# Small products in column tiles, a transfer of their own for search keys, and the next chunk's chain six ticks further forward

## What is computed

```python
xz = xseq @ in_proj_w; x, z = jnp.split(xz, 2, axis=-1)      # products xin, z
x = silu(conv1d(x))                                          # 4 taps per channel -> u
dt, Bm, Cm = split(x @ x_proj_w)                             # products dt, BC
delta = softplus(dt @ dt_proj_w + dt_proj_b)
h = exp(delta * A) * h + (delta * x) * Bm                    # the scan, 128 x 16 states
y = (einsum(h, Cm) + x * D) * silu(z) @ out_proj_w           # products y, out
# layer 1, on the image y
attn_c = softmax(xc @ xc.T); attn_s = softmax(q.T @ k)       # en; 4096 x 4096 scores
out = x + w_bn @ concat(attn_c @ x, v @ attn_s)
```

## Time and profile before

| | us |
|---|---|
| median of 3 runs | 8052.4 |
| lowest and highest | 8051.38, 8057.28 |
| the profiled execution | 8055.58 |
| its span, first to last instruction | 8053.8 |
| busy over the span: PE | 7258.6 (90%) |
| DVE | 6833.3 (85%) |
| ACT | 5958.7 (74%) |
| POOL | 3797.6 (47%) |

### The profile page before, as it was taken

The page is one execution under the profiler, slowest core; times in us unless marked ns, Lnnn a source line. Parts: engine busy times, 40 slices in busy tenths (PEclk is TensorE's granted clock), DMA queues, the critical chain, the costliest instruction groups (busy, mean ns, idle before and its releaser), DMA issues. The chain is left out here.

```text
span 8053.8 us, 226290 instructions
## 1 busy us (share of the span) xinstructions
PE 7258.6 (90%) x84718; PEld 2577.4 (32%) x84718; DVE 6833.3 (85%) x11132; ACT 5958.7 (74%) x10582; POOL 3797.6 (47%) x4135
## 2 busy tenths in 40 slices
PE   9972379999999999999989999999999999999998
PEld 2321123333333333333333333333333333333343
DVE  2228899898989899898989899898989899899987
ACT  1114478788888788887878788787878888788875
POOL 0016555555555455555545455555545455555500
PEclk9985589999999999999999999999999999999999
DMA  9838888888888888888888888878887888888820
GB/s 151 133 89 215 218 208 206 206 206 205 202 210 203 208 198 209 207 203 206 200 196 200 203 205 207 209 201 208 202 207 204 203 205 205 204 209 205 201 54 17
DMA packets 886811, 1535.68 MB, mean 191 GB/s; under 512 B 409480, under 2 KB 459472, under 8 KB 885712
## 3 DMA queue, kind: packets, MB, share of 16 engines
q1 hardware_dynamic: 882640, 1520.79, 78.3%
q10 hardware_dynamic: 3072, 0.40, 0.0%
HBM read 1326.69 MB, written 176.95 MB: 187 GB/s over the span
## 5 line engine op out<-in xcount | busy, mean ns | idle before, releaser
L1321 POOL TENSOR_TENSOR hst<-hst,cbc 128x512 f32<-128x512 f32 x2048 | 2623.1, 1281 | 2322.8 <-DVE bank L1179 2295.9
L1193 DVE TENSOR_TENSOR_SCAN hst<-dA,carry,bank 128x512 f32<-128x512 f32 x1792 | 2286.0, 1276 | 4.9 <-DVE bank L1179 0.4
L1044 ACT ACTIVATE pr<-bank 128x512 f32<-128x512 f32 x4096 | 2224.3, 602 | 36.7 <-PE bank L920 34.5
L931 PE MATMUL bank<-pr,vt 128*32 128x512 f32 x16384 | 2128.5, 595 | 2.3 <-DVE accs L1278 1.5
L1050 ACT ACTIVATE dA<-lanes,small 128x512 f32<-128x512 f32 x2048 | 1497.2, 731 | 645.7 <-DMA lanes<-spread_d 595.7
L917 PE MATMUL bank<-s1q,s1k 128*32 128x512 bf16 x16384 | 1626.6, 383 | 249.3 <-ACT pr L1044 151.1
L853 PE MATMUL bank<-s1kx,s1q 128*32 128x512 bf16 x16384 | 1641.2, 386 | 151.7 <-DMA s1kx<-kx_d 102.1
L986 ACT ACTIVATE gains<-bank 128x512 f32<-128x512 f32 x2048 | 1219.7, 596 | 650.0 <-PE bank L853 570.8
L1179 DVE TENSOR_TENSOR bank<-lanes,bbc 128x512 f32<-128x512 f32 x2048 | 1510.1, 737 | 200.2 <-DMA lanes<-spread_d 119.1
L920 PE MATMUL bank<-t2q,t2k 128*32 128x512 bf16 x16384 | 1616.5, 381 | 0.0
L1131 DVE CUSTOM_DVE_ANT_0 gains<-bank,gains 128x512 f32<-128x512 f32 x2048 | 1403.3, 685 | 210.6 <-PE bank L853 196.3
(11 more groups left out here) (120 smaller groups left out, 5757.9 us busy)
## 6 DMA issues: line engine op xcount, KB each, us to landing
lanes<-spread_d SPq DMA_DIRECT2D x2048, 512.0 KB, 6.3
seqt<-seq_d SPq DMA_DIRECT2D x256, 128.0 KB, 4.8
spread_d<-dsp SPq DMA_DIRECT2D x128, 256.0 KB, 2.0
spread_d<-usp SPq DMA_DIRECT2D x128, 256.0 KB, 2.0
bbc<-bc_d SPq DMA_DIRECT2D x128, 256.0 KB, 3.4
cbc<-bc_d SPq DMA_DIRECT2D x128, 256.0 KB, 4.0
xpad<-in_x SPq DMA_DIRECT2D x64, 256.0 KB, 6.7
ypad<-ypad SPq DMA_DIRECT2D x128, 128.0 KB, 4.2
```

The source lines that it names most:

```text
L931: mm = nc.tensor.matmul(ACC[CH * h + o:CH * h + o + BLOCK, :], vt[:, t, o:o + BLOCK], pr[:, T % PRING, h, :], start=t == 0, stop=t == KT - ...
L1044: nc.scalar.activation(pr[:, T % PRING, h, :], bank_of(("S", T, h))[:], ACT.Exp).then_inc(S["p_full"], 1)
L1193: nc.vector.tensor_tensor_scan(hst[:, slot_of(T), :], dA[:, T % 2, :], DBU[:], carry[:, g:g + 1] if sl % CHUNKS else 0.0, ALU.mult, ALU.ad ...
L1321: nc.gpsimd.tensor_tensor(h, h, cbc[:, (T - 1) // GROUPS % 2, :], ALU.mult).then_inc(S["hc_in"], 1)
```

## The change

- The products xin, z, dt, out, xv, en and res (the mix at the end of a quarter), each one matmul of 128 (en: 64) output rows, become matmuls of 32 output rows in separate column tiles of the array: four (en: two) where there was one.
- The front chain runs at (T + 6) % 16 instead of T % 16, so six ticks earlier; `u` gets three buffers instead of two. Its stores are put two steps later within the chain (at its step 12 instead of 10, 13 instead of 11) and the loads of bbc and cbc three (15 instead of 12).
- The search keys are stored at r = 12 instead of 14 under a semaphore of their own (`st_kx`), and the last quarter of `s1kx` is loaded at tick 14 instead of 16.
- After Ln, ACT runs an Exp on one column of a spare tile.
- Four small tiles become parts of `rest` and `low` that nothing else used, and the start takes six ticks more.

```diff
-SEARCH_LOAD = [SEARCH - KT + 8 * (p + 1) + 1 for p in range(QUARTERS - 1)] + [GROUPS]
+SEARCH_LOAD = [SEARCH - KT + 8 * (p + 1) + 1 for p in range(QUARTERS - 1)] + [GROUPS - 2]
...
+LEAD = 6
...
+        self.first = -GROUPS - LEAD if j == 0 else 0
...
-        for name in {0: ("xin", "z"), 6: ("dt",), 10: ("BC",)}.get(r, ()):
-            if self.chunk(sl + 1):
-                ev.append((name, sl + 1))
+        for name in {0: ("xin", "z"), 6: ("dt",), 10: ("BC",)}.get((T + LEAD) % GROUPS, ()):
+            c = (T + LEAD) // GROUPS + 1
+            if self.chunk(c):
+                ev.append((name, c))
...
-        u = sb("u", [P, 2, CHUNK])
+        u = sb("u", [P, 3, CHUNK])
...
+        nmx = rest[0:NT, 0:3 * P].rearrange("p (s n) -> p s n", n=P)
+        nm3 = low[0:NT, 0:3 * P].rearrange("p (s n) -> p s n", n=P)
+        energy = rest[0:CH, 3 * P:3 * P + CH]
+        catt = rest[0:CH, 3 * P + CH:4 * P]
...
+
+            def part_of(c):
+
+                return (c + CHUNKS * j) % 3
...
-                c = sl + 1
+                c, r = (T + LEAD) // GROUPS + 1, (T + LEAD) % GROUPS
...
-                                  (8, "ln_in"), (9, "delta_in"), (9, "du_in"), (10, "st_sp"),
-                                  (11, "st_bc"), (12, "ld_b"), (12, "ld_c")):
+                                  (8, "ln_in"), (9, "delta_in"), (9, "du_in"), (12, "st_sp"),
+                                  (13, "st_bc"), (15, "ld_b"), (15, "ld_c")):
...
-                        sl, r = T // GROUPS, T % GROUPS
-                        c = sl + 1
+                        c, r = (T + LEAD) // GROUPS + 1, (T + LEAD) % GROUPS
                         if r == 6 and sched.chunk(c + 2):
...
-                        if sched.chunk(c) and r == 10:
+                        if sched.chunk(c) and r == 12:
                             if due("delta_in", c):
                                 sp.wait_ge(S["delta_in"], due("delta_in", c))
                             issued(sp.dma_start(spread_d[c % 2, :, 0, :], dsp[:]), "st_sp")
...
-                        if sched.chunk(c) and r == 11:
+                        if sched.chunk(c) and r == 13:
...
-                        if sched.chunk(c) and r == 12:
+                        if sched.chunk(c) and r == 15:
                             wait(sp, "st_bc", c, 16 * BLOCKS)
                             wait(sp, "dbu_in", GROUPS * (c - 1) - 1)
...
+                            if r == 12:
+                                wait(sp, "mid_in", c)
+                                wait(sp, "head_in", c)
                                 for part, t in enumerate((head, mid)):
                                     issued(sp.dma_start(kx_d[bass.ds(i + a, 1), part].rearrange("a p l -> (a p) l")[:, cols],
-                                                        t[CH + QDIM:P, HALF:WIDE]), "st_split")
+                                                        t[CH + QDIM:P, HALF:WIDE]), "st_kx")
...
-                                wait(sp, "st_split", CHUNKS * a + stored, 80)
+                                wait(sp, "st_kx", CHUNKS * a + stored, 32)
                                 load_search(a, cols, f"ld_kx{p}")
...
-                            mm = nc.tensor.matmul(bank[:], mixw[:], x1a[:], start=True, stop=True)
+                            for o in range(0, P, BLOCK):
+                                mm = nc.tensor.matmul(bank[o:o + BLOCK, :], mixw[:, o:o + BLOCK], x1a[:],
+                                                      start=True, stop=True, tile_position=(0, o))
                         elif kind in ("xin", "z"):
                             wait(pe, f"seq{c % 2}", c, 32)
                             o = 0 if kind == "xin" else CH
-                            mm = nc.tensor.matmul(bank[:], win[o:o + CH, :], seqt[o:o + CH, c % 2, :],
-                                                  start=True, stop=True, tile_position=(o, 0))
+                            for b in range(0, P, BLOCK):
+                                mm = nc.tensor.matmul(bank[b:b + BLOCK, :], win[o:o + CH, b:b + BLOCK],
+                                                      seqt[o:o + CH, c % 2, :],
+                                                      start=True, stop=True, tile_position=(o, b))
                         elif kind == "dt":
                             wait(pe, "gated", c)
-                            mm = nc.tensor.matmul(bank[:], wdt[:], u[:, c % 2, :], start=True, stop=True)
+                            for o in range(0, P, BLOCK):
+                                mm = nc.tensor.matmul(bank[o:o + BLOCK, :], wdt[:, o:o + BLOCK], u[:, part_of(c), :],
+                                                      start=True, stop=True, tile_position=(0, o))
...
-                            mm = nc.tensor.matmul(bank[:], wout[:], ysb[:], start=True, stop=True)
+                            for o in range(0, P, BLOCK):
+                                mm = nc.tensor.matmul(bank[o:o + BLOCK, :], wout[:, o:o + BLOCK], ysb[:],
+                                                      start=True, stop=True, tile_position=(0, o))
...
                             for t in range(4):
-                                mm = nc.tensor.matmul(bank[:, t * P:(t + 1) * P], x1c[:, c % 2, t * P:(t + 1) * P],
-                                                      wxv[:], start=True, stop=True)
+                                for o in range(0, P, BLOCK):
+                                    mm = nc.tensor.matmul(bank[o:o + BLOCK, t * P:(t + 1) * P],
+                                                          x1c[:, c % 2, t * P + o:t * P + o + BLOCK], wxv[:],
+                                                          start=True, stop=True, tile_position=(0, o))
                         elif kind == "en":
                             taken(pe, ("xv", c))
                             for t in range(4):
-                                mm = nc.tensor.matmul(bank[0:CH, 0:CH], xv[:, t, 0:CH], xv[:, t, 0:CH],
-                                                      start=t == 0, stop=t == 3)
+                                for o in (0, BLOCK):
+                                    mm = nc.tensor.matmul(bank[o:o + BLOCK, 0:CH], xv[:, t, o:o + BLOCK],
+                                                          xv[:, t, 0:CH], start=t == 0, stop=t == 3,
+                                                          tile_position=(0, o))
...
-                        c = sl + 1
+                        c, r = (T + LEAD) // GROUPS + 1, (T + LEAD) % GROUPS
                         if sched.chunk(c) and r == 0:
...
-                            taken(act, ("y", c - 2))
-                            nc.scalar.activation(u[:, c % 2, :], cacc[:], ACT.Tanh).then_inc(S["tanh"], 1)
+                            taken(act, ("y", c - 3))
+                            nc.scalar.activation(u[:, part_of(c), :], cacc[:], ACT.Tanh).then_inc(S["tanh"], 1)
...
                             nc.scalar.activation(em1[:], em1[:], ACT.Ln).then_inc(S["ln_in"], 1)
-                        c = sl - 1
+                            nc.scalar.activation(spare[:, 1:2], spare[:, 0:1], ACT.Exp)
+                        c, r = sl - 1, T % GROUPS
...
-                            wait(act, "st_split", c - 1, 80)
+                            wait(act, "st_split", c - 1, 48)
+                            wait(act, "st_kx", c - 1, 32)
...
-                            nc.gpsimd.tensor_tensor(usp[:], dsp[:], u[:, c % 2, :], ALU.mult).then_inc(S["du_in"], 1)
+                            nc.gpsimd.tensor_tensor(usp[:], dsp[:], u[:, part_of(c), :], ALU.mult).then_inc(S["du_in"], 1)
```

More of the change, by code:

```diff
@@ L523, in _ @@
                 nc.vector.memset(mixw[:], 0.0)
+                nc.vector.memset(spare[:], 0.0)
                 nc.vector.memset(ones[:], 1.0).then_inc(zeroed, 1)
@@ L639, in span @@
                     sched.note(f"seq{c % 2}", c + 2)
-                elif T == sched.first == -GROUPS:
+                elif T == sched.first and T < 0:
                     sched.note("seq0", 0)
                     sched.note("seq1", 1)
-                c = sl - 1
+                c, r = sl - 1, T % GROUPS
                 if sched.chunk(c):
                     for at, n in ((4, "y2_in"), (8, "st_x1"), (8, "kd_in"), (9, "head_in"),
-                                  (10, "rest_in"), (11, "mid_in"), (12, "low_in"), (14, "st_split"), (13, "st_vt")):
+                                  (10, "rest_in"), (11, "mid_in"), (12, "low_in"), (12, "st_kx"), (14, "st_split"), (13, "st_vt")):
                         if r == at:
@@ L772, in _ @@
                                 wait(sp, "pv", (T - 2,))
-                                wait(sp, "st_split", CHUNKS * a + stored, 80)
+                                wait(sp, "st_split", CHUNKS * a + stored, 48)
                                 wait(sp, "st_vt", CHUNKS * a + stored, 16)
@@ L783, in _ @@
                             full_wait(sp, ("S", last_tick((a - 1, q)), 1))
```

(8 more changed lines are left out.)

20 lines of the change are left out of this document (8 added, 12 removed).

## The result

The changed kernel takes 7777.07 us (median of 4 runs, 7774.7 to 7780.85), the kernel before 8053.36 beside it: ratio 0.9657, interval 0.9640 to 0.9674, 276 us faster. The forecast was 7715. The time lies in the likeliest case's own range; the gain was 62 us smaller than forecast.

A forecast was written before the change was run, and what follows sets the result against it. In most ticks DVE was the limit, around the chunk's border PE. Savings of 190 (wait for y), 125 (keys) and 25 (lanes) less 3 (start) gave 337 us: 7718.6 profiled, so 7715; range 7610 to 7790, widened to 7600 to 7900.

The forecast's parts named there:

- likeliest case: The whole kernel takes 7715 us, own range 7610 to 7790, chance 0.58.
- the rivals: PE stays bound, 7810 to 7860, 0.15; lanes, 7925, 0.11; Ln pack behind y, 8155, 0.07; change ineffective, 8050, 0.04.
- The wait for y, 190 us: DVE's wait ahead of ysb, 2.3 us each, shrinks to 0.4, saving 190 us.
- The 0.95: Ahead of ysb, DVE has u, zs and two em operations instead of two taps, so it arrives 0.95 us later.
- The 0.55 on PE: Ahead of y, PE loses xin and z, gets tiled dt and a shorter en, so y comes 0.55 us earlier.
- The 0.4 for Ln: With Ln and its table loads beside y, PE arrives sooner still; 0.4 us of DVE's 2.3 us wait is left.
- the other 79: Remaining 79 us of DVE's waits for search products, ascribed to the ticks of the wait for y; 24 were left.
- Search keys, 125 us: Storing and loading the last search keys two ticks earlier, plus y's ticks, cuts DVE's waits for search products by 125 us.
- The 70 for the stall itself: DVE's 14 largest waits for search products, about 5 us each, go with PE's stall for the last search keys.
- SP and lanes, 25 us: SP's queue no longer waits for dsp, so a third of DVE's 73.6 us wait for lanes goes.
- no change for xin and z: The xin and z pair in 64 x 32 tiles was taken to stay at 1.16 us on PE.
- The 148 us of PE: Column tiles for dt, out, res, xv and en save PE 1.25 us a chunk, 148 us in 118 chunks.

The follow-up runs named there:

- no Ln: The kernel before with Ln replaced by Identity, leaving out both table loads of a chunk: 8045.6 us, ratio 1.0001.
- seven ticks: The changed kernel with the front chain seven ticks forward instead of six: 7705.9 us, ratio 0.9564.

## Why the prediction came out as it did

*Direction and rank of the cases.* Right, and the likeliest case was the nearest. None of the rivals decides: with the tiles alone worth nothing PE is not the bound; DVE's wait for lanes is 4.0 us; Ln cost nothing in the kernel before, and the place of its second table load costs nothing after. That the sum came near is in part luck. Held against the rows that its terms were read from, the wait for y fell by 23 us instead of 190, the wait for search products by 142 instead of 125, the wait for lanes by 70 instead of 25, and the first image, which the sum left out, gave 36.

*The wait for y, 190 us: the step that failed.* Its working was "y comes 0.55 earlier and DVE arrives 0.95 later", and then "lets PE arrive sooner still. I leave 0.4". The 0.95 was real in kind: DVE's work moved under its wait. It pays where it leaves, in half B (1.41 us), not as a shorter row: the row is 208.3 us against 230.8. The 0.55 on PE did not arrive: the tiles gave half A nothing alone, and 0.11 us with the chain. The 0.4 for Ln was nothing (no Ln, no gain). What comes late next was not asked: PE's own waits. PE and ACT now wait for DVE (the new rows above), and A is 0.30 longer. That the taps, now in ticks 11 to 13, are the cause is argued; no run moved them alone. An ordinary chunk gained 54.76 - 53.65 = 1.11 us, 131 us in 118 chunks, where the sum had 190, 25 and the 55 of "the other 79" in it, 270. (The stretch ends at the scan of T = 2046 and holds 1886 ticks, not the 1888 of the prediction; nothing hangs on it.)

*Search keys, 125 us.* 111 alone. The total was near, the split was not. The 70 for the stall itself came (68.5 with the keys alone), but the 55 from the ticks of y were not the keys' to give: the rest of their 111 came mostly out of the wait ahead of ysb. The row that had the price was the chunk's length, 8.1 x 14 = 113; DVE's own waits under-count a stall that PE passes on in several places.

*SP and lanes, 25 us.* Mis-sized. In the stretch the wait for lanes fell from 73.6 to 4.0, and the first image, which the sum left out, lost 36 us: before it DVE waited there for lanes too. The waits of DVE in the first image's scan, before and after:

```profile
DVE bank L1179 <- DMA lanes<-spread_d: 31.7, 18, 2.9
```

```profile
DVE bank L1203 <- DMA lanes<-spread_d: 0.2, 1, 0.2
```

The later steps of the stores were priced as a wait that goes. They and the later loads are what makes the forward chain pay at all: without them the changed kernel loses 578 us and is slower than the one before.

*Tiles, no change for xin and z, start +3.* The 148 us of PE were nearer in appearance than in fact: 150 us of busy time went, but only 113 by the tiles, the others with the keys and the chain. The pair takes 1.02, and the first scan starts at 588.4 instead of 588.7. That PE's time is not the kernel's was said; that only some 25 us would be had of it was not.

## What to carry to other kernels

Cut the period of a software pipeline where one engine hands the pace to the other, and read each half's busy times: work is worth something only where its engine has the pace, and moving an instruction pays at the place it leaves. A row of waits is not a price: a wait of an engine that is ahead (PE for Exp, 151 us) can vanish for nothing, and one that stays (DVE for y) can hold more work. When a producer moves forward, move the queue's stores of its result so that they still come after it; what stands behind them in that queue is the price.

## What the runs showed of the hardware

*PE's clock.* In the kernel before with tiles alone, PE's granted clock fell after PE had waited 0.68 and 1.29 us shortly one after the other about Ln. Its timeline, and the windows of that stretch and the one ahead:

```profile
2844.90 0.40 PE L929 MATMUL bank<-s1q,s1k 128*32 128x512 bf16 x4 [0.68 <-ACT gains L998]
2845.13 0.39 PE L932 MATMUL bank<-t2q,t2k 128*32 128x512 bf16 x4
2846.81 0.40 PE L929 MATMUL bank<-s1q,s1k 128*32 128x512 bf16 x4 [1.29 <-ACT pr L1056]
2847.04 0.59 PE L932 MATMUL bank<-t2q,t2k 128*32 128x512 bf16 x4
2847.40 0.65 PE L853 MATMUL bank<-s1kx,s1q 128*32 128x512 bf16 x4
2847.82 1.94 PE L943 MATMUL bank<-pr,vt 128*32 128x512 f32 x8
```

```profile
2840.00:2846.00 6.00, 4.83 (x64) 1.43 (x56) 5.87 (x11) 5.95 (x9) 3.20 (x4) 1.00 1.04 235
2846.00:2850.00 4.00, 3.19 (x24) 1.01 (x28) 3.93 (x8) 3.94 (x8) 2.13 (x3) 0.64 0.71 192
```

The granted clock was 0.64 over these 4 us, part of them at 1.2 GHz, and the values' product took 1.94 us instead of 1.03. This happened in 33 chunks there and at no such place in the kernel before, whose waits there are nearly always 0.40 and 1.29. But in 82 of the other 85 chunks of the same run the waits are as long as in the 33 (0.59 or 0.68, and 1.29), and the values' product is not slowed. So the waits alone do not decide it, and what does stays open. It cost little: those 33 chunks are 0.17 us longer than the same chunks before, the others 0.10 shorter.

*DVE beside POOL.* The changed kernel's timeline at `rq<-dq`:

```profile
3320.43 1.29 POOL L1345 TENSOR_TENSOR hst<-hst,cbc 128x512 f32<-128x512 f32 x1
3320.80 0.94 DVE L1307 TENSOR_TENSOR rq<-dq 128x8 f32<-128x8 f32 x1
```

DVE's operation begins while POOL's runs and ends 0.02 us after it. Of the 64 in that trace, the 58 that began beside a running POOL operation of this kind took 0.94 us (median), the other 6 took 0.16. The same holds for the operation that opens each tick (`bank<-lanes,bbc`): 1.29 us in 194 cases, 0.70 in the other 1854. The scan took 1.27 us beside POOL and 1.28 without. In the kernel before, no `rq<-dq` began so, but 128 operations on bank did and 112 of `rest<-x1c,head` (1.61 us against 1.06). An estimate from the traces, what such operations took above the median of the others, gives 137 us of DVE's time in the kernel before, 160 in the changed one and 106 with seven ticks: the order of DVE's operations sets this too.
